# Down-projections of six first-MLP units as 2x2 block multiplications with 7 products, two units adding up in the same banks, one operand kept in DRAM

## The chip, the cores and the metric

One core of one Trainium2 chip runs the whole program. The metric is the device time of one execution in microseconds, the median of several runs. TensorE (PE) multiplies, VectorE (DVE), ScalarE (ACT) and GpSimd (POOL) work on elements, and SyncE's queue (SP) issues almost all DMAs.

## What is computed

Two layers are applied to 32 sequences of 64 tokens, 512 features each. A layer is a block and then an adapter. The block, cut to what matters here:

```python
attn_out = softmax(q k^T * scale) v @ Wp + bp
cms_out  = gelu(attn_out @ cW1 + cb1) @ cW2 + cb2          # "first MLP", 512 -> 2048 -> 512
cms_out  = cms_out + one_hot(target_codes)
modifier = gelu(concat[attn_out, cms_out] @ mW1 + mb1) @ mW2 + mb2   # "second MLP", 1024 -> 2048 -> 512
out      = clip(x + cms_out + modifier, 0, 1)
```

The adapter picks one of three small two-layer networks by sequence, adds its input and normalises. Everything is float32. The kernel reaches that accuracy by splitting each operand into a rounded high part and the rest (HI and LO, type fp32r) and by adding three products, HI*HI, HI*LO and LO*HI, in PSUM.

## The kernel before

The sequences are done in two halves of 1024 tokens, each through two layers: four **passes**, p = 0 to 3. A pass is attention, then the two MLPs, then the adapter. In the MLPs the 2048 hidden features are cut into 8 groups of 256. A group of one MLP is a **unit**: units 0 to 7 belong to the first MLP, 8 to 15 to the second.

- **The up-projection** of a unit (`term`, `terms`) multiplies a 2x2 block matrix of weights with a 2x2 block matrix of tokens. It forms 7 products, P1 to P7, of sums and differences of blocks, instead of 8; units 0 and 8 (`plain`) use 8. A product is 6 matmuls of 128x512 in the first MLP, 12 in the second. ACT copies between banks (`copy_p1`, `copy_p5`, `copy_u2`) and DVE additions (`make_z22`, `make_z12`) put the products together. Two gelu instructions on ACT (`hidden`) write the high part and the raw value of each of four 128x512 blocks H00, H11, H10, H01, and DVE subtracts to get the low part.
- **The down-projection** of units 0 to 8 and 15 (`down`) is plain: 8 products of 6 matmuls, each into its own bank of the four in `d_out`, each added to `acc` by DVE (`add`, 128x512). Units 9 to 14 (`FAST`) use 7 products of 6 matmuls into double banks `d_a` and `d_b` (`fast_down`), with six additions of 128x1024 (`fast_add`), one ACT copy of a double bank (`copy_down`), and sums of hidden blocks (`hidden_sum`, with `split_sum` on ACT and `low_sum` on DVE for their parts) and of weight blocks (`combine_down` on POOL, `split_part` on ACT, `low_part` on DVE).
- **Weights** come by DMA, one unit ahead: `w1c` and `w1m` for the up-projection, `w2` for the down-projection. POOL forms the four weight sums of each unit (`combine`). ACT writes the high part (`weight_part`, `down_part`), DVE the low part.

Each engine runs its own list in the written order. PE alternates between the products of unit u and the down-projection of unit u-1 (`mlps`), so that others prepare one while it multiplies the other:

```python
terms(p, u, P1, P5, P6); down(p, u - 1, 0); terms(p, u, P2)
terms(p, u, P7);         down(p, u - 1, 1); terms(p, u, P4, P3)
```

SP waits for the low part of the last weight operand (P3) of unit u, loads the up-projection weights of unit u+1 over them, waits for the low part of the down-projection weights and loads those of unit u+1.

## Time and profile before

| | |
|---|---|
| median of 3 runs | 2037.12 us (2036.31 to 2037.77) |
| profiled execution | 2037.42 us |
| its span (first to last instruction) | 2035.5 us |
| granted TensorE clock over the span | 0.999 |
| busy: PE, PEld, DVE, ACT, POOL | 2021.2, 1692.2, 1508.2, 1021.5, 370.0 us |
| moved by DMA | 169.78 MB, 83 GB/s over the span |

PE is the matmul row, PEld the weight loads that run beside it. A busy PE is one that has matmuls in flight. The table of the chain that ended last gives PE 95% of the span, 88% of it to line 672, the matmuls of all projections. Line 1430 is DVE's helper for every low part, so its rows are told apart by the tile names: `hs` and `t` hidden blocks, `wsc` and `wsm` up-projection weights, `wd` and `wdp` down-projection weights.

### The profile page before, as it was taken

The numbers are of one execution on the slowest core, as the hardware profiler recorded it, in microseconds if no ns is written. First come the engines' busy times: TensorE is split into PE (matmuls) and PEld (weight loads), VectorE is DVE, ScalarE is ACT, GpSimd is POOL, SyncE is SP. The second block draws the span as 40 slices with busy tenths as digits, with TensorE's granted clock in tenths as the row PEclk, the third lists the DMA queues.
The fourth block names the chain that finished last, engine by engine and source line by source line (L and its number), as shares of the span: only waits on it lengthen the run. The fifth ranks groups of instructions, "written<-read, shape, count | busy, mean of one in ns | idle before, by whom it ended". The sixth has DMA issues, their size and how long they took to land.

```text
span 2035.5 us, 27682 instructions
## 1 busy us (share of the span) xinstructions
PE 2021.2 (99%) x9500; PEld 1692.2 (83%) x9500; DVE 1508.2 (74%) x2321; ACT 1021.5 (50%) x1844; POOL 370.0 (18%) x415
## 2 busy tenths in 40 slices
PE   9999999999999999999999999999999999999998
PEld 7888888888888888888888888888888888888887
DVE  7576677888767667888867666888886766778887
ACT  5464454555356444555435444555544544445552
POOL 0011112321101102232110110223210111032321
PEclk9999999999999999999999999999999999999999
DMA  8411211213411111112460121122252021211143
GB/s 292 166 32 42 73 47 63 73 59 113 161 68 42 52 65 60 48 62 73 155 234 22 51 63 67 37 73 73 71 189 104 11 62 42 78 62 47 62 145 95
DMA packets 42377, 169.78 MB, mean 83 GB/s; under 512 B 5624, under 2 KB 9720, under 8 KB 34808
## 3 DMA queue, kind: packets, MB, share of 16 engines
q1 hardware_dynamic: 42096, 167.97, 23.8%
q8 instruction: 80, 1.31, 0.3%
q14 instruction: 57, 0.47, 0.1%
q10 hardware_dynamic: 144, 0.03, 0.0%
HBM read 146.97 MB, written 21.01 MB: 83 GB/s over the span
## 4 chain that ended last, share of the span: by engine, by line
PE 95%; DMA 2%; DVE 2%; SPq 0%; issue 0%; POOL 0%; ACT 0%; DVEq 0%; ACTq 0%
PE psum L672 88%; DMA gains<-roles_in 1%; PE psum L966 1%; PE psum L1003 1%; PE psum L747 1%; PE psum L769 1%; DVE yt L1908 0%; PE psum L770 0%; PE psum L749 0%; SPq L422 0%; DMA fraw<-fuse_in 0%; PE psum L979 0%; PE psum L991 0%; DVE stats L1889 0%; PE psum L1015 0%
## 5 line engine op out<-in xcount | busy, mean ns | idle before, releaser
L672 PE MATMUL psum<-hs,wd 128*128 128x512 f32 x1920 | 448.8, 389 | 0.5
L672 PEld LDWEIGHTS psum<-hs,wd 128*128 128x128 f32 x1920 | 360.1, 188 | 76.9 <-DVE acc L1703 2.2
L672 PE MATMUL psum<-cop,wsm 128*128 128x512 f32 x1416 | 354.7, 389 | 0.0
L672 PE MATMUL psum<-aop,wsm 128*128 128x512 f32 x1320 | 333.0, 389 | 0.0
L672 PEld LDWEIGHTS psum<-cop,wsm 128*128 128x128 f32 x1416 | 265.8, 188 | 55.2
L672 PE MATMUL psum<-aop,wsc 128*128 128x512 f32 x1320 | 311.3, 389 | 0.0
L672 PEld LDWEIGHTS psum<-aop,wsm 128*128 128x128 f32 x1320 | 247.8, 188 | 51.4
L672 PEld LDWEIGHTS psum<-aop,wsc 128*128 128x128 f32 x1320 | 247.5, 188 | 51.4
L1679 DVE TENSOR_TENSOR acc<-psum,acc 128x1024 f32<-128x1024 f32 x144 | 175.6, 1219 | 87.2 <-PE psum L672 87.1
L1703 DVE TENSOR_TENSOR acc<-psum,acc 128x512 f32<-128x512 f32 x256 | 167.9, 684 | 84.5 <-PE psum L672 84.4
L1430 DVE TENSOR_TENSOR hs<-hs_raw,hs 128x512 fp32r<-128x512 f32 x256 | 178.8, 706 | 43.5 <-ACT hs_raw L1243 43.5
L1242 ACT ACTIVATE hs<-psum,bias 128x512 fp32r<-128x512 f32 x120 | 82.1, 684 | 237.2 <-PE psum L672 237.1
L672 PE MATMUL psum<-hs,wdp 128*128 128x512 f32 x576 | 146.2, 389 | 0.0
L1242 ACT ACTIVATE hs<-zt,bias 128x512 fp32r<-128x512 f32 x112 | 81.0, 723 | 113.7 <-PE psum L672 71.7
L672 PEld LDWEIGHTS psum<-hs,wdp 128*128 128x128 f32 x576 | 108.1, 188 | 22.4
L1171 ACT ACTIVATE wsm<-w1m 128x512 fp32r<-128x512 f32 x156 | 96.1, 622 | 37.0 <-DMA w1m<-m_in 37.0
L1430 DVE TENSOR_TENSOR wsm<-w1m,wsm 128x512 fp32r<-128x512 f32 x156 | 110.3, 723 | 1.3 <-ACT wsm L1171 1.0
L672 PE MATMUL psum<-t,wdp 128*128 128x512 f32 x432 | 109.6, 389 | 0.0
L1685 DVE TENSOR_TENSOR zt<-psum,zt 128x512 f32<-128x512 f32 x56 | 38.7, 691 | 80.2 <-PE psum L672 80.2
L609 POOL TENSOR_TENSOR comb<-w1c 128x256 f32<-128x256 f32 x28 | 20.7, 738 | 416.2 <-DMA w1c<-c_in 416.2
L672 PEld LDWEIGHTS psum<-t,wdp 128*128 128x128 f32 x432 | 81.1, 188 | 16.8
L616 POOL TENSOR_TENSOR w1m<-w1m,comb 128x512 f32<-128x512 f32 x28 | 45.4, 1620 | 269.8 <-DVE wsm L1430 269.8
(193 smaller groups left out, 3072.9 us busy)
## 6 DMA issues: line engine op xcount, KB each, us to landing
w1m<-m_in SPq DMA_DIRECT2D x32, 1024.0 KB, 4.9
w1c<-c_in SPq DMA_DIRECT2D x32, 512.0 KB, 3.5
w<-c_in SPq DMA_DIRECT2D x32, 512.0 KB, 3.6
w<-m_in SPq DMA_DIRECT2D x32, 512.0 KB, 3.5
gains<-roles_in SPq DMA_DIRECT2D x30, 512.0 KB, 5.1
fw<-fused SPq DMA_DIRECT2D x6, 2048.0 KB, 10.3
fused<-fw SPq DMA_DIRECT2D x4, 2048.0 KB, 7.6
xmid<-x SPq DMA_DIRECT2D x4, 2048.0 KB, 6.8
```

The lines of the kernel that those rows point to most:

```text
L609: nc.gpsimd.tensor_tensor(st, w_block(u, 1, 0), w_block(u, 1, 1), ALU.add).then_inc(w1_sums, 1)
L616: nc.gpsimd.tensor_tensor(w_block(u, 0, 1), w_block(u, 0, 1), st, ALU.subtract).then_inc(w1_sums, 1)
L672: mm = nc.tensor.matmul(out, lhs(a), rhs(b), start=(start and n == 0), stop=(stop and n == total - 1), skip_group_check=reopened)
L747: nc.tensor.matmul(out, tq[:, j // 2, HI, j % 2, i * P:(i + 1) * P], xs[:, :, j, tile], start=(j == 0), stop=False)
L769: nc.tensor.matmul(out, val[:, HI, v_cols], val[:, :, p_cols], start=True, stop=False)
L966: nc.tensor.matmul(out, tokens, wdn_flat[:, bass.ds(role * (2 * KC * BN) + (c * KC + k) * BN, BN)], start=(b == 0 and k == 0 and a == c), ...
L1171: nc.scalar.activation(slot(u, i)[:, HI, :], w_source(u, i), ACT.Copy).then_inc(s_hi[i], 1)
L1242: nc.scalar.activation(hs[:, b, HI, m, :], h_source(h, u), ACT.Gelu, bias=b1)
L1430: return nc.vector.tensor_tensor(out, a, hi.bitcast(F32), ALU.subtract)
L1679: nc.vector.tensor_tensor(dst, bank, dst, ALU.add).then_inc(acc_done, 1)
L1685: nc.vector.tensor_tensor(zt[:, 2, :], bank_b()[:, :], zt[:, 2, :], ALU.add).then_inc(z22_done, 1)
L1703: nc.vector.tensor_tensor(dst, d_out[o][:, :], dst, ALU.add).then_inc(acc_done, 1)
```

## The change

- **Pairs.** Units 1 to 6 form three pairs (1,2), (3,4), (5,6), `PAIRED`. The down-projections of a pair are done together in the 7-product form: each of 7 products takes 12 matmuls (2 banks, 2 units, 3 parts), both units adding up in the same double bank. The six additions to `acc`, the copy and the bank turns are done once for a pair.
- **Room.** The hidden operands of two units of a pair stand in `pairs`, over the area of `cop`. One operand of that area (`x12`, attention output kept for unit 8) goes to DRAM (`kept`) in unit 0 and comes back after the last pair. The weight operands of a pair turn through 7 slots, `wdc`, in an area that unit 8's plain weights use after them. A second raw buffer `w2b` holds the odd unit's down weights; SP loads both units' raw weights together.
- **POOL** gets 4 sums per unit for the down weights, two of them formed in the slot itself (`pair_first`, `pair_last`).
- **Order.** PE's list is written anew for units 1 to 7. The lists of ACT and DVE for these units are written out one item after the other (`first_units`, 166 and 201 items); only their first lines stand here. The second MLP is as before. The softmax's five semaphores become one counter, with the same waits.
- **SP** waits for all seven low parts before it overwrites weights. Before unit 8's `w1m`, it also waits for the last pair's low parts and loads `w2` of unit 7 first.

```diff
+PAIR_DOWN = (P5, P3, P1, P6, P2, P7, P4)
+PAIRED = range(1, NG - 1)
+PAIR_SLOTS = 7
...
+        def group(u):
+            return ((u, u + 1) if u % 2 else (u - 1, u)) if paired(u) else (u,)
...
+            if paired(u):
+                return 7 * (group(u)[0] - 1) + 2 * down_turn(u, i) + (u % 2 == 0)
...
@@ SP, one_pass
                         else:
-                            sp.wait_ge(s_lo[P3], strassen(p, u) + 1)
+                            for i in range(7):
+                                sp.wait_ge(s_lo[i], units(p, u, i) + 1)
+                        if u + 1 == NG:
+                            sp.wait_ge(d_lo, d_at(p, u))
+                            load_w2(u)
                         load_w1(u + 1)
...
+                    if paired(u):
+                        if u in (4, 6):
+                            sp.wait_ge(d_lo, d_at(p, u - 1))
+                            for v in group(u):
+                                load_w2(v)
+                    elif u == 0:
+                        sp.wait_ge(d_lo, d_at(p, u + 1))
+                        load_w2(2)
+                        sp.wait_ge(x12_lo, 2 * p + 1)
+                        sp.dma_start(kept, x12_flat).then_inc(x12_stored, 16)
+                    else:
+                        sp.wait_ge(d_lo, d_at(p, u + 1))
+                        if u == NG - 1:
+                            sp.wait_ge(dn_done, dn_at(p, u))
+                            sp.wait_ge(x12_stored, 16 * (p + 1))
+                            sp.dma_start(x12_flat, kept).then_inc(x12_back, 16)
...
@@ POOL
+            def pair_first(p, u):
+                for v in group(u):
+                    pool.wait_ge(*w2_here(p, v))
+                    nc.gpsimd.tensor_tensor(w2_block(v, 2, 1), w2_block(v, 1, 1), w2_block(v, 2, 1), ALU.subtract).then_inc(w2_sums, 1)
+                    pool.wait_ge(w2_sums, w2_sum(p, v, P7))
+                    nc.gpsimd.tensor_tensor(part_source(v, P6), w2_block(v, 2, 2), w2_block(v, 2, 1), ALU.subtract).then_inc(w2_sums, 1)
+            def pair_last(p, u):
+                for i in (P5, P3):
+                    for v in group(u):
...
+                        elif u in (5, 7):
+                            combine_first(p, u)
+                            pair_first(p, u - 1)
+                            combine_last(p, u)
+                            pair_last(p, u - 1)
...
@@ PE, fast_down
+                        pe.wait_ge(acc_done, {P5: a0 - (2 if behind(u) is None else 1), P3: a0 + 1, P1: a0 + 2, P7: a0 + 3, P4: a0 + down_turn(u, P7)}[i])
...
+                        mm = product(out[:, o, :], [(lambda a, v=v: part(v, i)[:, a, o * P:(o + 1) * P],
+                                                     lambda c, v=v: h_operand(v, i, c), None) for v in us], first, True, not first)
...
@@ PE, mlps
-                    if fast(u - 1):
+                    if u in (1, 2):
+                        terms(p, u, P1, P5, P6)
+                        down(p, 0, u - 1, 0, 1)
+                        terms(p, u, P2, P7)
+                        down(p, 0, u - 1, 2, 3)
+                        terms(p, u, P4, P3)
+                    elif u in (3, 5):
+                        terms(p, u, P1, P5, P6)
+                        fast_down(p, u - 1, P5)
+                        terms(p, u, P2, P7)
+                        fast_down(p, u - 1, P3)
+                        terms(p, u, P4, P3)
+                    elif u in (4, 6):
+                        terms(p, u, P1)
+                        fast_down(p, u - 2, P1)
+                        terms(p, u, P5, P6)
+                        fast_down(p, u - 2, P6)
+                        terms(p, u, P2)
+                        fast_down(p, u - 2, P2)
+                        terms(p, u, P7)
+                        fast_down(p, u - 2, P7)
+                        terms(p, u, P4, P3)
+                        fast_down(p, u - 2, P4)
+                    elif u == NG - 1:
+                        terms(p, u, P1, P5, P6)
+                        fast_down(p, u - 1, P5)
+                        terms(p, u, P2)
+                        fast_down(p, u - 1, P3)
+                        terms(p, u, P7)
+                        fast_down(p, u - 1, P1)
+                        terms(p, u, P4)
+                        fast_down(p, u - 1, P6, P2, P7)
+                        terms(p, u, P3)
+                        fast_down(p, u - 1, P4)
...
@@ ACT, weight_part
                 if u == NG:
+                    act.wait_ge(dn_done, dn_at(p, NG - 2) + down_turn(NG - 2, {P6: P2, P7: P7, P2: P4, P4: P4}[i]) + 1)
...
@@ DVE
+            def first_units(p, layer):
+                weight_part(p, 1, P4)
+                weight_part(p, 1, P3)
+                add(p, layer, 0, 0, 0)
+                make_z22(p, 1)
...
```

How PE's list stands in unit 7 of pass 0, before. The `aop,wsc` rows are up-projection products (6 matmuls: a first one with its waits, then 5), the `hs,wd` rows the plain down-projection of unit 6.

```order
L672 MATMUL psum<-aop,wsc 128x512 [waits p1_copied,s_lo1]
L672 MATMUL psum<-aop,wsc 128x512 x5
L672 MATMUL psum<-aop,wsc 128x512 [waits u2_copied,s_lo6]
L672 MATMUL psum<-aop,wsc 128x512 x5
L672 MATMUL psum<-hs,wd 128x512 [waits h_lo3,acc_done]
L672 MATMUL psum<-hs,wd 128x512 x2
L672 MATMUL psum<-hs,wd 128x512 [waits h_lo1]
L672 MATMUL psum<-hs,wd 128x512 x2
L672 MATMUL psum<-hs,wd 128x512 [waits acc_done]
L672 MATMUL psum<-hs,wd 128x512 x5
```

The same place after the change: the pair product P5 of units 5 and 6 (12 matmuls), then P2 of unit 7, then the pair product P3.

```order
L831 MATMUL psum<-pairs,wdc 128x512 [waits ht_lo,d_lo,acc_done]
L831 MATMUL psum<-pairs,wdc 128x512 x2
L831 MATMUL psum<-hs,wdc 128x512 x3
L831 MATMUL psum<-pairs,wdc 128x512 x3
L831 MATMUL psum<-hs,wdc 128x512 x3
L831 MATMUL psum<-aop,wsc 128x512 [waits p1_copied,s_lo1]
L831 MATMUL psum<-aop,wsc 128x512 x5
L831 MATMUL psum<-pairs,wdc 128x512 [waits h_lo0,d_lo,acc_done]
```

Six matmuls now stand between a pair product and the next one that waits for `acc_done`, DVE's addition of it; before, several products of other banks lay between such a wait and what it waits for.

SP's list from the load of unit 7's up-projection weights on, before:

```order
L483 DMA w1c<-c_in 128x1024 [waits s_lo2]
L487 DMA w_52<-c_in 128x1024 [waits d_lo]
L481 DMA w1m<-m_in 128x2048 [waits s_lo2]
L487 DMA w_52<-m_in 128x1024 [waits d_lo]
L481 DMA w1m<-m_in 128x2048 [waits s_lo3]
```

And after the change (`w_52` is `w2`; the first row stands for the loads of units 6 and 7):

```order
L583 DMA w1c<-c_in 128x1024 [waits s_lo4,s_lo3,s_lo5,s_lo2,s_lo6,s_lo1,s_lo0] x2
L587 DMA w2b<-c_in 128x1024 [waits d_lo]
L587 DMA w_52<-c_in 128x1024
L587 DMA w_52<-c_in 128x1024 [waits s_lo4,s_lo5,s_lo3,s_lo6,s_lo2,d_lo,s_lo1,s_lo0]
L581 DMA w1m<-m_in 128x2048
L660 DMA cop<-kept 128x2048 [waits x12_stored,dn_done,d_lo]
L587 DMA w_52<-m_in 128x1024
L581 DMA w1m<-m_in 128x2048 [waits s_lo3]
```

The load of unit 8's `w1m` moved behind `d_lo`, the low part of the last weight operand of pair (5,6), and behind a load of `w2`; the return of `kept` is new, ahead of unit 8's `w2`.

## Rows read from the trace of the kernel before

**Rows 1.** The page: busy time of the engines, and the granted clock in 40 slices.

```profile
PE 2021.2 (99%) x9500; PEld 1692.2 (83%) x9500; DVE 1508.2 (74%) x2321; ACT 1021.5 (50%) x1844; POOL 370.0 (18%) x415
...
PEclk9999999999999999999999999999999999999999
```

**Rows 2.** The chain that ended last, pass 0: start us, us, what.

```profile
121.92 380.81 PE psum L672 x1680
```

**Rows 3.** Who PE waited for, whole span: us in total, times, longest us.

```profile
PE psum L991 <- DVE hz L1430: 3.6, 4, 1.6
PE psum L679 <- POOL ident L581: 1.5, 1, 1.5
```

**Rows 4.** Stretches of pass 0: units 1 to 7, then units 8 to 15.

```profile
core 0: us, PE busy (x) PEld busy (x) DVE busy (x) ACT busy (x) POOL busy (x), PEclk, DMA share, GB/s
121.92:264.55 142.63, 142.63 (x630) 118.12 (x630) 95.98 (x159) 70.96 (x136) 19.47 (x25) 1.00 0.17 52
264.55:502.70 238.15, 238.15 (x1052) 197.28 (x1051) 191.28 (x260) 125.50 (x219) 60.92 (x53) 1.00 0.22 76
```

**Rows 5.** DVE in order of time, unit 11: start us, us, what [idle before].

```profile
378.08 0.42 DVE L1430 TENSOR_TENSOR wdp<-comb,wdp 128x256 fp32r<-128x256 f32 x1
378.42 0.68 DVE L1430 TENSOR_TENSOR wsm<-comb,wsm 128x512 fp32r<-128x512 f32 x1
379.02 1.22 DVE L1679 TENSOR_TENSOR acc<-psum,acc 128x1024 f32<-128x1024 f32 x1
380.15 0.60 DVE L1430 TENSOR_TENSOR wdp<-w,wdp 128x256 fp32r<-128x256 f32 x1
```

**Rows 6.** PE in order of time, unit 10 and the end of unit 15.

```profile
342.07 1.52 PE L672 MATMUL psum<-t,wdp 128*128 128x512 f32 x6
343.43 1.52 PE L672 MATMUL psum<-aop,wsm 128*128 128x512 f32 x6
...
498.47 11.50 PE L672 MATMUL psum<-hs,wd 128*128 128x512 f32 x48
```

**Rows 7.** PEld in order of time, the same two places.

```profile
343.21 1.32 PEld L672 LDWEIGHTS psum<-aop,wsm 128*128 128x128 f32 x6
...
504.20 1.93 PEld L672 LDWEIGHTS psum<-hs,wd 128*128 128x128 f32 x9 [0.55 <-DVE acc L1703]
```

**Rows 8.** DVE in order of time, the same two places.

```profile
343.70 1.22 DVE L1679 TENSOR_TENSOR acc<-psum,acc 128x1024 f32<-128x1024 f32 x1 [2.11 <-PE psum L672]
...
503.45 2.49 DVE L1703 TENSOR_TENSOR acc<-psum,acc 128x512 f32<-128x512 f32 x4
```

**Rows 9.** ACT in order of time, units 11 and 12.

```profile
377.71 0.40 ACT L1194 ACTIVATE wdp<-w 128x256 fp32r<-128x256 f32 x1
...
383.20 0.63 ACT L1199 ACTIVATE t<-t_raw 128x512 fp32r<-128x512 f32 x1 [0.24 <-DVE t_raw L1665]
...
396.67 1.01 ACT L1205 ACTIVATE psum<-psum 128x1024 f32<-128x1024 f32 x1 [0.24 <-PE psum L672]
```

**Rows 10.** POOL in order of time, first and second MLP.

```profile
171.12 0.74 POOL L609 TENSOR_TENSOR comb<-w1c 128x256 f32<-128x256 f32 x1 [12.75 <-DMA w1c<-c_in]
...
290.06 2.21 POOL L613 TENSOR_TENSOR comb<-comb,w1m 128x512 f32<-128x512 f32 x1 [15.56 <-DVE wsm L1430]
```

**Rows 11.** DVE in order of time, at the second POOL row.

```profile
289.90 1.22 DVE L1430 TENSOR_TENSOR cop<-cop_raw,cop 128x1024 fp32r<-128x1024 f32 x1
291.04 1.78 DVE L1430 TENSOR_TENSOR hs<-hs_raw,hs 128x512 fp32r<-128x512 f32 x1
```

**Rows 12.** The page, DMA issues: KB each, median us to landing.

```profile
w1m<-m_in SPq DMA_DIRECT2D x32, 1024.0 KB, 4.9
...
w<-c_in SPq DMA_DIRECT2D x32, 512.0 KB, 3.6
...
xmid<-x SPq DMA_DIRECT2D x4, 2048.0 KB, 6.8
```

**Rows 13.** SP's queue in order of time, the load for unit 8.

```profile
249.24 0.33 SPq L481 DMA_DIRECT2D w1m<-m_in  x1
```

More of the change, by code:

```diff
@@ new lines, in part_at, with w2_block, w2_odd, w2_here @@
+        def part_at(p, u, i):
+            if paired(u):
+                return d_at(p, group(u)[1]) + 2 * down_turn(u, i) + (u % 2 == 0) + 1
+            return d_at(p, u) + down_turn(u, i) + 1
+        def w2_block(u, half, chunk):
+            return (w2b if w2_odd(u) else w2)[:, (2 - chunk) * V + (half - 1) * 2 * P:(2 - chunk) * V + half * 2 * P]
+        def w2_odd(u):
+            return paired(u) and u % 2 == 1
+        def w2_here(p, u):
+            loads = [v for v in range(u + 1) if w2_odd(v) == w2_odd(u)]
+            per_pass = sum(w2_odd(v) == w2_odd(u) for v in range(UNITS))
+            return w2b_loaded if w2_odd(u) else w2_loaded, 16 * (per_pass * p + len(loads))
@@ L790, in block_products @@
                     pe.wait_ge(s_lo[PLAIN[m, k]], n + 1)
-                    if b == 0:
+                    if kind and which == 0 and b and k == 0:
+                        pe.wait_ge(x12_back, 16 * (p + 1))
+                    elif b == 0:
                         pe.wait_ge(op_lo[(P1, P2)[k]], 2 * p + which + 1)
@@ L866, in down @@
                         pe.wait_ge(acc_done, acc_at(p, u) + o + 1)
-                    elif fast(u - 1):
+                    elif behind(u) is not None:
                         pe.wait_ge(acc_done, acc_at(p, u) - (o < 2))
@@ L1308, in second_unit @@
+            def mlps(p, layer):
+                first_unit(p, layer, 0)
+                first_units(p, layer)
+                first_unit(p, layer, 1)
+                for u in range(NG + 1, UNITS):
+                    second_unit(p, layer, u)
             def second_unit(p, layer, u):
@@ L1783, in second_unit @@
+            def mlps(p, layer):
+                first_unit(p, layer, 0)
+                first_units(p, layer)
+                first_unit(p, layer, 1)
+                for u in range(NG + 1, UNITS):
+                    second_unit(p, layer, u)
             def second_unit(p, layer, u):
```

687 lines of the change are left out of this document (542 added, 145 removed).

## Prediction

> **What bounds the kernel now.** I read the page first: PE is busy for 99% of the span at the full granted clock [rows 1]. A busy PE need not be a bound one, so I next read the chain in order of time. The reader should see one unbroken piece of PE in pass 0, from 121.92 us, 380.81 us long, of 1680 matmuls; the other three passes show a piece of the same length and count [rows 2]. That is units 1 to 15 but for the last two thirds of unit 15's down-projection. It gives 380.81/1680 = 0.2267 us for each matmul, with nothing else in it. The waits say the same: the largest of PE's is 3.6 us in the whole run, in the adapter [rows 3]. So in the MLPs a matmul saved is 0.2267 us saved, as long as the others still deliver in time. The stretches show what room they have: in units 1 to 7 PE runs 630 matmuls in 142.63 us, beside 95.98 us of DVE, 70.96 of ACT and 19.47 of POOL [rows 4].
>
> **What is removed.** A plain down-projection is 48 matmuls, a share in a pair is 42. Six units in four passes: 6 x 6 x 4 = 144 matmuls, 144 x 0.2267 = **32.6 us**, all on the path. Units 1 to 7 become 594 matmuls, 134.7 us a pass.
>
> **What DVE gets.** Starts that follow each other directly show what an instruction occupies: 0.34 us for 256 columns, 0.60 for 512, 1.13 for 1024 [rows 5]. By the new list, units 1 to 7 hold 86 of 256 columns (44 parts of up weights, 42 of down weights), 96 of 512 (8 additions, 14 z blocks, 24 sums of hidden blocks, 24 and 22 low parts, 4 parts for unit 8) and 19 of 1024 (18 additions, one weight block). That is 29.2 + 57.6 + 21.5 = 108.3 us in 134.7, 80%. It fits, and from each item that waits for a PE product to the next one that PE needs, the sum of the items between stays under PE's time between, except at the places priced below. Cost nothing, cover 26 us a pass; if that is gone, DVE becomes the bound (rival 3).
>
> **What ACT gets.** Add 42 casts of 256 columns at 0.40, 24 of 512 at 0.63 and 3 copies at 1.01 [rows 9] to the 70.96 us: 106 us at most (the six weight casts and six gelus it loses are left in), 79% of 134.7. Hidden. POOL: 28 sums as before and 24 new, 52 x 0.74 = 38.5 us [rows 10]. Hidden as work; what it does to DVE is rival 3.
>
> **What is added on the path: four short turns in unit 7.** The last pair has only unit 7 to hide in. There the pair products P5, P3 and P1 are 6 matmuls apart, and so are P7 and P4. Each of these waits for DVE's addition of the product before it in the same double bank (P6 waits for ACT's copy of P1). Unit 10 shows how long such a turn takes. A 6-matmul product starts at 342.07 and the next one at 343.43 [rows 6]; its addition starts at 343.70, 0.27 later, and lasts 1.22 [rows 8]. At the end of unit 15 a weight load starts 0.06 us after an addition ends (503.45 plus 0.69 for the first of four, then 504.20) [rows 7, 8]. A weight load runs 0.22 us ahead of its matmul (343.21 against 343.43) [rows 6, 7]. Together 0.27 + 1.22 + 0.06 + 0.22 = 1.77 us, and 6 matmuls cover 1.36: 0.41 us late, three times. With the copy (0.24 after its product, 1.01 long [rows 9]) it is 1.53 against 1.36: 0.17. Sum 1.4 us a pass, **5.6 us**. The bounds: nothing, if the modelled ends are late by that much, and 0.55 a turn, the idle time of the one real stall of this kind [rows 7], 8.8 us. I take 5.6, since that stall costs its row of 48 matmuls 11.50 - 11.04 = 0.46 us [rows 6] and the same sum of steps explains it. Elsewhere pair products have 12 or more matmuls, or other banks, in between: nothing.
>
> **The gate of unit 8.** SP now loads `w1m` of unit 8 behind the low part of the last pair operand, whose slot comes free only when pair product P6 ends. From there: 0.27 to ACT, 0.40 and 0.42 for the two parts [rows 5, 9], some 0.4 to issue two loads, then 1.5 MB. The 1 MB load alone takes 4.9 us, 2 MB take 6.8 [rows 12]; I take 6.5. Then two casts and two low parts of 512, some 2.0. That is 10.0 us. PE reaches unit 8 after P2, P7, P3 of unit 7 and P4: 42 matmuls, 9.5 us, plus 0.4 for P4's turn. Before, the load was issued at 249.24 [rows 13], 15 us ahead. Nearly even: late by 0 to 2 us a pass; I take 0.3, **1.2 us**. The next items (unit 8's other two parts, unit 7's last hidden blocks and its weight block) follow within 0.5 us of their time each, no more.
>
> **The operand in DRAM.** 1 MB out in unit 0, waited for by the gelu of H10 in unit 1, some 20 us later; 1 MB back, issued once unit 7's weight block is split, some 5 us after the last pair product, and needed 72 matmuls (16.3 us) after it. The nearest loads take 4.9 and 6.8 us [rows 12]: hidden with 4 us to spare. If it came late, unit 8 would wait for the excess, 0 to 2 us a pass. Moved loads of `w2` arrive 5 us before POOL needs them for pairs (3,4) and (5,6); the load of unit 8's `w2` is 5 us later than before and 15 us early. The softmax's one counter for five changes no wait: nothing.
>
> **Small lateness.** Lists this full, in fixed order, will now and then hold an item that PE waits for behind one that is waiting itself (the copy of P1 in unit 5 behind a weight part that hangs on POOL, for one). Nothing in the trace of before prices it: from below nothing, from above the 26 us that DVE has free being used up, which is rival 3. I take 0.5 us a pass, **2.0 us**, near the lower end, since before DVE is 80% busy in units 8 to 15 (191.28 of 238.15 [rows 4]) and PE loses nothing there.
>
> **Sum.** 32.6 - 5.6 - 1.2 - 2.0 = 23.8. The profiled execution took 2037.4 us (its span is 2035.5; it stands 0.3 above the median of the runs): **2013.5 us**.
>
> **Rival 1: all of it is hidden.** The turns cost nothing because a matmul's end is modelled, and the load arrives. For it: 1680 matmuls without a gap under the same kinds of waits [rows 2]. Against it: the stall at 504.20 [rows 7]. 2037.4 - 32.6 = 2004.8 us.
>
> **Rival 2: full lists, more waiting.** The cross waits of ACT, DVE and POOL cost 3 us a pass instead of 0.5, and the load for unit 8 is 1.5 us late. 2004.8 + 5.6 + 12 + 6 = 2028 us.
>
> **Rival 3: DVE becomes the bound, by POOL's reads.** At 290.06 a POOL addition starts inside DVE's 1.22 us low part at 289.90, which runs its normal time; the POOL one takes 2.21 us, and DVE's next low part, from 291.04, takes 1.78 instead of 0.68 [rows 5, 10, 11]. So one waits for the other, and DVE loses 1.1 us to an instruction of 1.3. If each of the 52 POOL sums of units 1 to 7 cost DVE its full 0.74 us, DVE would need 108.3 + 38.5 = 146.8 us where PE took 142.63 before: 4.2 us a pass longer, 17 us in all, **2054 us, slower**. The point from which it decides is 69% of POOL's time lost by DVE (26.4 of 38.5 us), and slower than before from 89%. Against it: an addition that reads PSUM beside POOL keeps its time, nearly a third of DVE's new time is of that kind (8 + 14 instructions of 512 and 18 of 1024), and before, DVE kept 80% busy without PE losing any. The Trainium skill, page "SBUF — State Buffer", section on who interferes with whom, says that the shared ports are an exclusive lock: a DVE instruction with both inputs in SBUF and a GpSimd one that reads SBUF block each other fully, whoever came first. By that rule, and the trace agrees (2.21 and 1.78 us), each such meeting costs what rival 3 takes; the rule alone says nothing of how often they meet.
>
> **Rival 4: a load in the new SP order is far too late.** SP is one queue, and it now waits for down weights before up weights. If the return of `kept` or unit 8's weights came 6 to 8 us late in each pass, the gain would be gone: 2035 to 2041 us. Against it, the sums above leave it 0 to 2.
>
> **How the numbers follow.** The forecast with its own range of 2008 to 2020 has 0.47, rival 1 (2003 to 2008) 0.24, rival 2 (2020 to 2033) 0.18, rival 4 0.04, rival 3 0.07. The predicted time is the likeliest case, 2013.5. With 2 in 10 left out, the range runs from 2004, rival 1 with its full saving, to 2027, most of rival 2. 0.2% is 4 us, about what a measurement of this kernel can tell from no change. Faster by more: 0.89, which is the forecast with rivals 1 and 2; within it: 0.03, most of rival 4; slower: 0.08, rival 3 and the end of rival 4.
>
> **What the profile of the changed kernel would show.** PE has 144 matmuls fewer, 9356. The long piece of each pass falls from 380.81 us to some 375, broken in unit 7. Weight loads before pair products P3, P1 and P4 of unit 7 are idle by 0.3 to 0.6 us, released by DVE's 1024 additions, and P6's by ACT's copy. DVE is 80 to 90% busy in units 1 to 7. If PE shows no idle time there, rival 1 holds. If its idle time is released by DVE low parts all over units 3 to 7, and these last longer than 0.42 and 0.68 us beside POOL, it is rival 3. If it is released by the DMA of `w1m` or of `cop`, it is the gate or rival 4. A time above 2027 or below 2004 makes the prediction wrong.

## The result, and the profile after

| | before | after |
|---|---|---|
| median of the runs, us | 2036.8 (2036.31 to 2037.77, 4 runs) | 2024.47 (2023.48 to 2025.08, 4 runs) |
| profiled execution: time, span, us | 2037.4, 2035.5 | 2024.03, 2022.3 |
| PE's matmuls | 9500 | 9356 |
| DVE busy, us | 1508.2 (74%) | 1631.7 (81%) |

The ratio is 0.9937, 95% interval 0.9923 to 0.995: faster by 12 us, where 32.6 us of matmuls went. 2013.5 was forecast and the stated range, 2004 to 2027, held; of the 23.8 us of gain that I had taken as likeliest, about half came. One of the four runs of version e10 further down took 3774.6 us at a granted clock of 0.831, where all others had 0.998 or more; e10's ratio leaves it out (the other three: 2011.34 to 2012.03, median 2011.44), its median of 2011.74 does not. The page after, beside [rows 1]:

```profile
PE 1998.4 (99%) x9356; PEld 1662.8 (82%) x9356; DVE 1631.7 (81%) x2513; ACT 1104.6 (55%) x2072; POOL 472.6 (23%) x511
...
PEclk9999999999999999999999999999999999999999
```

The clock is as before. The chain that ended last (start us, us, what) was one piece of 380.81 us [rows 2]. Now, in pass 0 and at the start of pass 1's second MLP:

```profile
130.92 5.77 PE psum L831 x24
141.32 42.48 PE psum L831 x186
197.42 42.49 PE psum L831 x186
239.96 4.34 PE psum L831 x18
244.35 13.94 PE psum L831 x60
258.35 241.00 PE psum L831 x1062
...
743.51 7.03 DMA w1m<-m_in
```

From 258.35, where the last pair product P4 starts, PE runs on unbroken; all that is lost in pass 0 is lost in units 1 to 7. From the start of unit 1 to PE's restart at the end of unit 15, the passes took 382.28 us each before (121.92 to 504.20 in the first), and take 378.67, 379.84, 378.62 and 378.45 now. That is 3.61, 2.44, 3.66 and 3.83 us less, 13.5 in all, where 36 matmuls less should give 8.16 each.

PE's weight loads show where (pass 0; start us, us, what [idle ahead of it <- what ended it]):

```profile
130.92 1.23 PEld L831 LDWEIGHTS psum<-aop,wsc 128*128 128x128 f32 x6 [1.04 <-DVE wsc L1786]
...
141.32 1.22 PEld L831 LDWEIGHTS psum<-aop,wsc 128*128 128x128 f32 x6 [0.99 <-DVE wsc L1786]
...
189.55 2.61 PEld L831 LDWEIGHTS psum<-pairs,wdc 128*128 128x128 f32 x12 [0.74 <-issue]
...
195.27 1.23 PEld L831 LDWEIGHTS psum<-aop,wsc 128*128 128x128 f32 x6 [0.39 <-issue]
197.39 0.53 PEld L831 LDWEIGHTS psum<-hs,wdc 128*128 128x128 f32 x3 [0.90 <-DVE wdc L1786]
...
239.93 0.53 PEld L831 LDWEIGHTS psum<-pairs,wdc 128*128 128x128 f32 x3 [0.44 <-issue]
...
258.31 0.53 PEld L831 LDWEIGHTS psum<-pairs,wdc 128*128 128x128 f32 x3 [0.44 <-issue]
```

0.04 us of each idle time is the usual step from load to load. These are, in order: unit 1 before P7; unit 2 before P6; the pair product P4 of (1,2), which waits for DVE's addition of the pair product P7; unit 5's P6; the pair product P5 of (3,4); and two of unit 7's turns (a turn is the change of a double bank from one product to the next). A load can run ahead of its matmul, so PE itself loses a little less. By the starts of its matmuls against 0.2267 us each, pass 0 loses 1.77 us in units 1 and 2, 1.67 in units 4 and 5, 1.07 in unit 7: 4.51 us, and 8.16 - 4.51 = 3.65 is the gain of pass 0. The first five places are in all four passes. Unit 8's load costs 1.24 us in pass 1 (the DMA piece in the chain above) and nothing in the others.

At the same place before, DVE's three low parts of unit 1 stood like this (start us, us, what):

```profile
129.68 1.08 DVE L1430 TENSOR_TENSOR wsc<-w1c,wsc 128x256 fp32r<-128x256 f32 x3
```

And now, with POOL beside them:

```profile
128.28 1.71 DVE L1786 TENSOR_TENSOR aop<-aop_raw,aop 128x1024 fp32r<-128x1024 f32 x1 [0.19 <-ACT aop L1331]
129.92 2.71 DVE L1786 TENSOR_TENSOR wsc<-w1c,wsc 128x256 fp32r<-128x256 f32 x3
```

```profile
128.87 1.71 POOL L765 TENSOR_TENSOR w2b<-w2b 128x256 f32<-128x256 f32 x1
130.66 0.80 POOL L767 TENSOR_TENSOR comb2p<-w2b 128x256 f32<-128x256 f32 x1
...
135.29 0.75 POOL L779 TENSOR_TENSOR wdc_raw<-w,comb2p 128x256 f32<-128x256 f32 x1
```

Three low parts of 256 columns took 1.08 us before; they take 2.71 beside the pair sums, which POOL forms in one burst of eight. The third of them is the weight operand of P7, and all seven must be done before SP loads unit 2's weights. In units 4 and 5 the burst runs from 184.75 to 195.3, and there DVE is busy 31.13 of 32.00 us (stretch, us, then PE, PEld, DVE, ACT, POOL with counts, clock, DMA):

```profile
183.00:215.00 32.00, 31.16 (x136) 24.88 (x135) 31.13 (x49) 23.01 (x49) 13.30 (x13) 1.00 0.14 48
```

The two theories to part. T1: POOL's sums, which read SBUF, stretch DVE's instructions with two SBUF inputs, and that makes the stalls of units 1, 2, 4 and 5. T2: no collision is needed; PE's new order and fuller lists are enough.

### The profile page after: what moved, and what is told of

The parts are those of the page before. It is cut to its first block, busy times and chain, and to the rows that moved or that the text cites. A ratio compares the mean times of both kernels' runs of the same rounds, so it can differ in the third digit from the quotient of the medians.

```text
span 2022.3 us, 28718 instructions
## 1 busy us (share of the span) xinstructions
PE 1998.4 (99%) x9356; PEld 1662.8 (82%) x9356; DVE 1631.7 (81%) x2513; ACT 1104.6 (55%) x2072; POOL 472.6 (23%) x511
## 4 chain that ended last, share of the span: by engine, by line
PE 90%; DVE 4%; DMA 2%; issue 1%; ACT 1%; SPq 1%; POOL 1%; DVEq 0%; ACTq 0%
PE psum L831 83%; PE psum L1160 1%; DMA gains<-roles_in 1%; PE psum L1197 1%; PE psum L906 1%; PE psum L928 1%; DVE wsc L1786 1%; DVE pairs_raw L2022 0%; DVE yt L2454 0%; PE psum L1173 0%; DMA fraw<-fuse_in 0%; PE psum L929 0%; PE psum L908 0%; SPq L522 0%; DVE pairs L1786 0%
## 5 line engine op out<-in xcount | busy, mean ns | idle before, releaser
L2038 DVE TENSOR_TENSOR acc<-psum,acc 128x1024 f32<-128x1024 f32 x216 | 263.4, 1220 | 103.2 <-PE psum L831 102.7
L831 PE MATMUL psum<-aop,wsc 128*128 128x512 f32 x1320 | 319.9, 390 | 5.0 <-DVE wsc L1786 4.8
L831 PE MATMUL psum<-hs,wd 128*128 128x512 f32 x768 | 181.3, 390 | 0.5
L831 PE MATMUL psum<-pairs,wdc 128*128 128x512 f32 x672 | 177.0, 392 | 1.7 <-DVE acc L2038 1.1
L831 PEld LDWEIGHTS psum<-hs,wd 128*128 128x128 f32 x768 | 143.9, 188 | 32.2 <-DVE acc L2062 2.2
L831 PEld LDWEIGHTS psum<-pairs,wdc 128*128 128x128 f32 x672 | 124.5, 188 | 34.0 <-issue 8.2
L1786 DVE TENSOR_TENSOR hs<-hs_raw,hs 128x512 fp32r<-128x512 f32 x192 | 133.4, 707 | 11.4 <-ACT hs_raw L1446 11.4
L1445 ACT ACTIVATE hs<-psum,bias 128x512 fp32r<-128x512 f32 x80 | 54.9, 687 | 88.0 <-PE psum L831 87.8
L734 POOL TENSOR_TENSOR comb<-w1c 128x256 f32<-128x256 f32 x28 | 26.1, 932 | 300.8 <-DMA w1c<-c_in 300.7
L831 PE MATMUL psum<-fw,xs 128*128 128x512 f32 x384 | 93.1, 395 | 0.0
```

Of the source, the lines that this page charges most:

```text
L734: nc.gpsimd.tensor_tensor(st, w_block(u, 1, 0), w_block(u, 1, 1), ALU.add).then_inc(w1_sums, 1)
L831: mm = nc.tensor.matmul(out, lhs(a), rhs(b), start=(start and n == 0), stop=(stop and n == total - 1), skip_group_check=reopened)
L1445: nc.scalar.activation(h_high(u, h), h_source(h, u), ACT.Gelu, bias=b1)
L1786: return nc.vector.tensor_tensor(out, a, hi.bitcast(F32), ALU.subtract)
L2038: nc.vector.tensor_tensor(dst, bank, dst, ALU.add).then_inc(acc_done, 1)
```

## The experiments

In the expectations, P1 to P7 are called parts. The last column sums all idle time ahead of PE's weight loads in the four MLP stretches, beyond 0.04 us each: 22.5 us for the change, of which PE itself loses 19.1.

| run | median (range), us | ratio to before, 95% | idle, us |
|---|---|---|---|
| the change | 2024.47 (2023.48 to 2025.08) | 0.9937, 0.9923 to 0.995 | 22.5 |
| e1_write_only | 2014.68 (2012.6 to 2017.12) | 0.9894, 0.9879 to 0.991 | 10.3 |
| e2_pool_later | 2031.49 (2029.41 to 2032.93) | 0.9969, 0.9957 to 0.9981 | 32.4 |
| e3_unit1_order | 2027.92 (2025.86 to 2030.3) | 0.9958, 0.9944 to 0.9971 | 24.5 |
| e4_halves | 2022.85 (2022.7 to 2024.7) | 0.9933, 0.9919 to 0.9946 | 19.6 |
| e5_early_sums | 2023.25 (2020.05 to 2023.56) | 0.9926, 0.9913 to 0.994 | 18.5 |
| e6_vector_sums | 2025.61 (2024.26 to 2028.11) | 0.9945, 0.9931 to 0.9958 | 22.5 |
| e7_cover | 2025.94 (2024.08 to 2027.81) | 0.9944, 0.9931 to 0.9958 | 24.4 |
| e8_together | 2017.42 (2016.66 to 2017.75) | 0.9901, 0.9886 to 0.9916 | 14.7 |
| e9_lists | 2012.71 (2011.9 to 2013.82) | 0.9881, 0.9866 to 0.9896 | 8.1 |
| e10_pool_sums | 2011.74 (from 2011.34) | 0.9875, 0.9857 to 0.9894 | 8.3 |
| e11_lists45 | 2023.11 (2022.12 to 2025.55) | 0.9934, 0.992 to 0.9947 | 21.1 |
| e12_last_wait | 2012.16 (2009.75 to 2013.86) | 0.9878, 0.9861 to 0.9894 | 8.0 |

Intervals are some 3 us to each side, so differences of 2 us between neighbours rest on the trace and not on the time.

**Sums that read nothing.** In `pair_first` and `pair_last`:

```diff
-nc.gpsimd.tensor_tensor(part_source(v, P6), w2_block(v, 2, 2), w2_block(v, 2, 1), ALU.subtract).then_inc(w2_sums, 1)
+nc.gpsimd.memset(part_source(v, P6), 0.0).then_inc(w2_sums, 1)
...
```

> POOL's eight pair sums of each pair of units are written as constants (memsets), so they read nothing from SBUF; the sums of the down-projection's weights are left out of what is computed. Waits, order and counts of instructions stay. In the profile of the changed kernel TensorE loses 4.5 us in a pass: 1.77 in units 1 and 2, 1.67 in units 4 and 5, 1.07 at the turns of unit 7. Theory T1, the stalls of units 1, 2, 4 and 5 come from POOL's pair sums that read SBUF beside VectorE's low parts and stretch them (0.42 us to 0.9): with nothing read they go but for about 0.45 a pass that is due to the order of unit 1 alone, so 3.0 a pass and 12 us less, about 2012.5 us, with the turns of unit 7 unchanged at 1.07. Rival T2, the order of TensorE's products and the fuller lists alone make VectorE late: the stalls stay within 1 us a pass of what they are and the time is 2021 to 2025 us.

2014.68 us, 9.8 less; the idle time falls by 12.2 us. POOL's memsets and DVE's three low parts beside them:

```profile
130.13 0.57 POOL L777 MEMSET wdc_raw<- 128x256 f32 x2
130.63 0.57 POOL L779 MEMSET wdc_raw<- 128x256 f32 x2
```

```profile
129.94 1.08 DVE L1786 TENSOR_TENSOR wsc<-w1c,wsc 128x256 fp32r<-128x256 f32 x3
```

1.08 us again, with POOL writing all the while. SP issues unit 2's load at 131.16 instead of 132.76. The waits of units 4 and 5 are gone altogether; of 1.00 and 0.95 in units 1 and 2, 0.47 and 0.72 stay; the turns are unchanged. T1 holds, and T2 keeps a share of 1.2 us a pass. A memset is also shorter than a sum (0.3 against 0.74 us), so the time alone can't tell reading from length; the unstretched low parts beside running memsets can. The Trainium skill, page "SBUF — State Buffer", section "Who interferes with whom", says just this: a DVE instruction with two SBUF inputs meets a GpSimd instruction that reads SBUF, not one that only writes it. The trace agrees, 1.08 against 2.71 us.

In units 4 and 5 the same 22 instructions of DVE, from the z block at 183.83 in the change up to the addition at 199.03, can be laid side by side. First the change, then e1:

```profile
183.83 0.69 DVE L2044 TENSOR_TENSOR zt<-psum,zt 128x512 f32<-128x512 f32 x1
...
185.23 1.04 DVE L1786 TENSOR_TENSOR t<-zt,t 128x512 fp32r<-128x512 f32 x1
...
187.34 0.96 DVE L1786 TENSOR_TENSOR wsc<-w1c,wsc 128x256 fp32r<-128x256 f32 x1
```

```profile
183.07 0.69 DVE L2044 TENSOR_TENSOR zt<-psum,zt 128x512 f32<-128x512 f32 x1
...
184.47 0.69 DVE L1786 TENSOR_TENSOR t<-zt,t 128x512 fp32r<-128x512 f32 x1
...
186.18 0.42 DVE L1786 TENSOR_TENSOR wsc<-w1c,wsc 128x256 fp32r<-128x256 f32 x1
...
195.69 1.21 DVE L2038 TENSOR_TENSOR acc<-psum,acc 128x1024 f32<-128x1024 f32 x1
```

From the z block's start to the start of that addition (199.03 and 195.69) it is 15.20 us in the change and 12.62 in e1, though e1 has 0.41 us of idle time in it and the change none above 0.15. So DVE did not wait for POOL's results there: its own instructions were longer beside the sums, by more than the 1.90 us that PE waited.

**The burst later.** POOL's sums of pair (1,2) go behind unit 2's combinations, the splits of its part 5 with them:

```diff
                         if u == 1:
                             combine(p, u)
-                            pair_first(p, u)
-                            pair_last(p, u)
+                        elif u == 2:
+                            combine(p, u)
+                            pair_first(p, u)
+                            pair_last(p, u)
```

> Everything is computed. POOL forms the sums of pair (1, 2) behind unit 2's combinations of weights instead of ahead of them, and the split of that pair's part 5 on ACT and VectorE moves behind those of unit 1, directly ahead of unit 2's own. T1 (collision in the burst beside unit 1): the burst at 128 to 136 us no longer meets unit 1's low parts, the combinations of unit 2 and ACT's copies come earlier, and of the 1.77 a pass in units 1 and 2 some 1.3 go, 5 us in all, about 2019.5 us; units 4 and 5 keep their 1.67. T2 (order alone): 0 to 1 us less. A third outcome: the burst meets the low parts of unit 2 or 3 instead and the stalls only move, 2022 to 2026 us.

2031.49 us, 7 more: the third outcome, and worse than its bound. Units 1 and 2 keep 0.46 and 0.72 as in e1, but the burst (139.68 to 147.9) now meets the low parts that unit 3 and the first pair need:

```profile
143.76 1.22 DVE L1788 TENSOR_TENSOR pairs<-pairs_raw,pairs 128x512 fp32r<-128x512 f32 x1
```

```profile
150.99 5.29 PEld L833 LDWEIGHTS psum<-aop,wsc 128*128 128x128 f32 x24 [1.55 <-issue]
157.01 1.22 PEld L833 LDWEIGHTS psum<-aop,wsc 128*128 128x128 f32 x6 [0.72 <-issue]
```

1.22 us where 0.68 is normal. From 139.3 to 150 us DVE has no idle time above 0.15 us in which it could make this up; in unit 1 of the change it had some (0.33 us before 135.35 and 0.56 before 136.60).

**Unit 1 in the old order.**

```diff
-                        down(p, 0, u - 1, 0, 1)
-                        terms(p, u, P2, P7)
-                        down(p, 0, u - 1, 2, 3)
+                        down(p, 0, 0)
+                        terms(p, u, P2, P7)
```

> Everything is computed. In unit 1 alone TensorE's order is the one of before: all four outputs of unit 0's last down product between parts 6 and 2, where the change has two there and two later, which brings part 7 forward by 12 matmuls or 2.7 us. T1: VectorE's third low part is in time again in spite of its 2.71 us beside POOL (it was 0.91 late with 2.7 to gain), so the 0.91 goes, and with it the load that waits for it comes up to 0.9 earlier and unit 2's 0.86 goes for the most part: 5 to 7 us less in all, 2017.5 to 2019.5 us. T2 gives the same here; if neither order nor collision is the cause, nothing changes (2023 to 2025 us). The stretch of VectorE's low part beside POOL (2.71 us) stays, which tells cause from cover.

2027.92 us, 3.5 more: a miss for all I expected. P7's wait is gone, but another stands in its place, before P4 (PE's load, then DVE's addition that it waits for):

```profile
136.53 5.29 PEld L831 LDWEIGHTS psum<-aop,wsc 128*128 128x128 f32 x24 [1.72 <-issue]
```

```profile
135.77 0.69 DVE L2048 TENSOR_TENSOR zt<-psum,zt 128x512 f32<-128x512 f32 x1 [1.68 <-ACT zt L1416]
```

P7 goes through ACT's copy and DVE's z22 before its bank is free for P4: 1.7 us, ending at 136.46. Before, this stood behind 24 down matmuls of unit 0; in the change units 1 and 2 have 24 each instead of 48, since their pair's down work comes later. So the edit was no undoing of the order: half of what covered the two gaps is no longer there, and it can cover one or the other.

**The turns in halves.** For the last pair, DVE's additions of P5, P3 and P7 and ACT's copy are made in two halves of 512, and PE waits for each half:

```diff
+nc.vector.tensor_tensor(dst[:, 0, :], bank[:, 0, :], dst[:, 0, :], ALU.add).then_inc(acc_first, 1)
+nc.vector.tensor_tensor(dst[:, 1, :], bank[:, 1, :], dst[:, 1, :], ALU.add).then_inc(acc_done, 1)
```

> Everything is computed. In the last joint pair alone, VectorE's three additions of parts 5, 3 and 7 into the partial results and ACT's copy of the banks are made in two halves of 512 columns, each with its own signal, and TensorE waits for each half before it writes that half. If the turns of unit 7 cost what the changed kernel's profile shows (1.07 us a pass: 0.30 or so at each of three waits for VectorE and 0.05 at ACT's copy), the waits for the first half end about 0.6 us earlier and all of it goes: 4.3 us less, about 2020.2 us. If TensorE's idle time there is only a wait that would be paid again behind it, at the next turn, the time stays at 2023 to 2025 us. The stalls of units 1, 2, 4 and 5 stay.

2022.85 us, 1.6 less, not 4.3. The idle time at the turns is gone in all passes, but PE is then earlier at unit 8, and in three of four passes it waits for the weights there, by 0.26, 1.90 and 1.39 us where it was 0, 1.24 and 0 (the second of them):

```profile
751.59 2.38 PEld L832 LDWEIGHTS psum<-aop,wsm 128*128 128x128 f32 x11 [1.94 <-issue]
```

The idle time falls by 2.9 us in all. So the turns do cost what PE's starts say, and half of it is paid again at the gate, the load for unit 8.

**The burst earlier.** In unit 0 POOL waits 26 us and DVE's list is thin:

```diff
-                            combine(p, u)
+                            combine_two(p, u)
                             pair_first(p, u)
                             pair_last(p, u)
+                            combine_third(p, u)
+                            combine_last(p, u)
```

> Everything is computed. POOL forms the eight sums of pair (1, 2) in unit 0, between its second and third combination for unit 1 (after 91 us, where it waits 26 us in the changed kernel and VectorE's list is thin), instead of at 128 us beside unit 1's low parts. T1 (collision): unit 1's third low part takes 1.1 us again instead of 2.7, the load behind it is issued at 131.2 us as with sums that read nothing, and the stalls of units 1 and 2 go from 0.91 and 0.86 to what that run kept, 0.47 and 0.72: 0.6 to 0.8 a pass, 2.4 to 3.2 us in all, about 2021.5 us. T2 (order and full lists, no collision): no change, 2023 to 2025 us. The 0.47 and 0.72 that stay are the share of the order in both.

```profile
130.28 1.24 PEld L841 LDWEIGHTS psum<-aop,wsc 128*128 128x128 f32 x6 [0.50 <-DVE wsc L1796]
```

The low parts take 1.08 us again, SP issues at 131.04, and units 1 and 2 lose 0.46 and 0.72, within 0.01 us what e1 kept. The idle time falls by 4.0 us, 3.1 of them in units 1 and 2. The median says 1.2 less, which by its number is T2's case; the span of the profiled execution says 3.1 (2019.2). That is too little to show in the time, and the trace decides. It is the same collision taken away with everything computed. As the whole burst is gone from unit 1, this run by itself does not part POOL's reads from its length; e1's low parts beside memsets do.

**Four sums of pair (3,4) on DVE.**

```diff
@@ POOL
-                            pair_last(p, u - 1)
+                            if u == 7:
+                                pair_last(p, u - 1)
...
@@ DVE
                 weight_part(p, 5, P2)
+                pair_sums(p, 4)
                 hidden_sum(p, 4, P5)
```

> Everything is computed. The last four of the eight sums of pair (3, 4), parts 5 and 3, are made by VectorE (0.42 us each, 1.7 in all) behind its low part of unit 5's part 2, instead of by POOL at 191 to 195 us. T1: VectorE pays 1.7 us of its own but its neighbours keep their nominal times (0.95 back to 0.42 twice, 1.23 to 0.68, 1.83 to 1.2 for a pair), so units 4 and 5 lose about 0.6 to 0.8 a pass instead of 1.67, since the first four sums on POOL still meet VectorE ahead of them: 3.5 to 4 us less, about 2020.5 us. T2 (VectorE's list is simply too full there): 1.7 us more on it make the stalls of units 4 and 5 longer by up to 1.7 a pass, 2025 to 2031 us.

2025.61 us: no gain, T2's case by its number. The pair product's wait is gone (0.85), but unit 5's P6 waits 1.35 instead of 0.35, since ACT's queue stands behind a hidden sum that DVE reaches later:

```profile
192.50 0.63 ACT L1394 ACTIVATE pairs<-pairs_raw 128x512 fp32r<-128x512 f32 x1 [3.69 <-DVE pairs_raw L2023]
```

DVE's own four sums, 1.7 us by their nominal times and 2.2 here, cost as much as the collision that they replace.

**One output on each side of P7**, in units 1 and 2:

```diff
-                        terms(p, u, P2, P7)
-                        down(p, 0, u - 1, 2, 3)
+                        terms(p, u, P2)
+                        down(p, 0, u - 1, 2)
+                        terms(p, u, P7)
+                        down(p, 0, u - 1, 3)
```

> Everything is computed. In units 1 and 2 the last two outputs of unit 0's down-projection are no longer both between parts 7 and 4: one stands ahead of part 7 (6 matmuls, 1.36 us), one stays behind it. The run with four outputs ahead of part 2 and none behind part 7 showed a wait of 1.68 us ahead of part 4, with nothing to cover it. If each gap is a matter of how many matmuls of the down-projection stand ahead of it, part 7 is no longer late (0.91 and 0.86 gone) and part 4 waits 1.68 less 1.36, 0.3 each: 1.2 less a pass, 4.7 us in all, about 2019.8 us. If the delay is only handed on (VectorE is late through the unit, whatever PE does), the time stays at 2023 to 2027 us.

2025.94 us. P7 and P4 of unit 1 wait no more, but unit 2 waits three times instead of once, 2.06 us in place of 0.95, and unit 3 once, 0.35:

```profile
136.45 1.23 PEld L831 LDWEIGHTS psum<-aop,wsc 128*128 128x128 f32 x6 [0.57 <-DVE wsc L1788]
137.93 1.22 PEld L831 LDWEIGHTS psum<-aop,wsc 128*128 128x128 f32 x6 [0.26 <-DVE wsc L1788]
140.50 1.22 PEld L831 LDWEIGHTS psum<-aop,wsc 128*128 128x128 f32 x6 [1.35 <-DVE wsc L1788]
```

DVE's three low parts still take 2.72 us here, so unit 2's weights come late, and PE only meets them sooner. The delay is handed on, as long as the collision stands.

**Together.** e5, e6, e7 and e4, and at SP:

```diff
                         if u + 1 == NG:
-                            sp.wait_ge(d_lo, d_at(p, u))
-                            load_w2(u)
+                            sp.wait_ge(d_lo, part_at(p, 5, P4))
                         load_w1(u + 1)
+                        if u + 1 == NG:
+                            sp.wait_ge(d_lo, d_at(p, u))
+                            load_w2(u)
```

> Everything is computed. The last three edits and the halves of the turns together, and the load of unit 8's weights of part 1 ahead of that of unit 7's down weights, so that it is issued 1 us earlier. If the causes add up, a pass loses 0.6 in units 1 and 2, 0.6 in units 4 and 5, nothing at the turns and under 0.5 at the load of unit 8, in place of 4.5: about 2010 to 2012 us, which would beat the changed kernel by 0.6 to 0.7%. If the edits get in each other's way (VectorE's list holds more instructions in unit 7 and 4), 2016 to 2022 us.

2017.42 us, the second case: 7 us less, and 7.8 us less of idle time. The places say which edits gave it. The turns' idle time is gone, 5.7 us, and with the load issued earlier unit 8 takes only 0.3 more; so e4's gain now stays. Units 1 to 3 have 3.6 us less, of which e5 alone gave 3.1. Units 4 to 6 have 1.2 more. So e6 and e7, which gave nothing alone, give little or nothing here too: with the burst gone, the split cover takes away unit 1's last wait, 0.46 us a pass, but 0.35 appears in unit 3, and in units 4 and 5 a pass loses 2.06 us where the change loses 1.90.

**With the lists mended.** On top of that four list entries moved, DVE's four sums parted two and two, and the outputs parted in unit 1 alone. Three of the moves:

```diff
+                weight_part(p, 2, P5)
                 hidden_sum(p, 1, P5)
-                weight_part(p, 2, P5)
...
-                weight_part(p, 5, P1)
                 fast_add(p, 2, P7)
+                weight_part(p, 5, P1)
...
+                copy_p1(p, 5)
                 split_part(p, 3, P5)
...
-                copy_p1(p, 5)
                 split_part(p, 3, P3)
```

> Everything is computed. As the version of all edits together (2017.4 us, still 3.6 us lost a pass: 0.73 ahead of unit 2's part 6, 0.36 in unit 3, 0.71 behind unit 4's part 7, 1.36 ahead of unit 5's part 6, 0.42 at unit 8), with the moves that its profile asks for. VectorE's low part of unit 2's part 5, on which POOL's third combination and so part 6 waits, goes ahead of a sum of hidden units; its low part of unit 5's part 1 goes behind the addition of part 7; its own four sums of pair (3, 4) are parted two and two; ACT's copy of part 1's bank in unit 5 goes ahead of two copies that wait for those sums; ACT's copy of unit 7's down weights goes behind two of unit 8's; the two outputs are parted in unit 1 alone. If each wait is made by the list entry ahead of it, all five go: 2 to 3.5 us a pass, 2004 to 2009 us. If they are only handed to the next wait (VectorE as the bound of these units), 2012 to 2018 us.

> Everything is computed. As the kernel before it in this call, but the sums of pair (3, 4) are all POOL's again, as in the change. If the collision of POOL's sums with VectorE is what makes part 5 of that pair late, 0.85 a pass comes back there (3.4 us more than the run with VectorE's sums). If only the order of the lists mattered, the two are within 1 us of each other, or this one is faster by VectorE's 1.7 us a pass where that list is full.

2012.71 and 2011.74 us, the second case of e9's expectation: the waits of units 2, 3, 5 and 8 fall from 0.73, 0.36, 1.36 and 0.42 to 0.26 and nothing in pass 0, that of 0.70 before the pair product P4 of (1,2) goes too, and one of 1.42 is left, before the pair product P5 of (3,4). It is 1.42 with DVE's sums and with POOL's. So e10's second case holds: who forms those four sums makes no difference here. Either way DVE is as full: it is busy for 31.20 of the 32 us from 183 to 215 in e9, and 31.39 in e10. e10 is the fastest in this study with e12, 0.9875 against the change's 0.9937, 0.6% below it.

**Two list entries alone**, on the change as it was (the last two moves above):

> Everything is computed. The changed kernel with two moves alone, both at units 4 and 5, and POOL's sums where they are: VectorE's low part of unit 5's part 1 behind its addition of part 7, and ACT's copy of part 1's bank in unit 5 ahead of the copies that wait for POOL's sums. If the 0.70 and 0.35 a pass there are made by the entries ahead of them, which the collision stretched, they go and the 0.85 ahead of the pair's part 5 stays or grows by some of it: 0.5 to 1.05 a pass, 2 to 4 us less, 2020.5 to 2022.5 us. If VectorE is simply too full there, nothing changes (2023 to 2026 us).

2023.11 us. The 0.70 and 0.35 go and 0.85 becomes 1.44: of 1.90 us of idle time in units 4 and 5 of pass 0, 0.46 is won and the rest is handed to the next product. The time is that of the second outcome, the trace shows the first.

**The last wait.** On top of e10, for pair (3,4):

```diff
+                low_sum(p, 4, P5)
                 low_part(p, 3, P5)
-                hidden(p, 3, H00)
                 low_part(p, 4, P5)
-                low_sum(p, 4, P5)
+                hidden(p, 4, H11)
+                hidden(p, 3, H00)
```

> Everything is computed. As the fastest version so far (2011.7 us, POOL's sums of pair (3, 4) where the change has them, 1.68 us lost in pass 0), with moves at its largest wait, 1.42 us a pass ahead of pair (3, 4)'s part 5: VectorE's low half of the summed hidden units for part 5 and its two low parts of that part's weights go ahead of the low halves of two other blocks of hidden units (1.22 us and 0.68 us), and ACT copies the second unit's part 5 ahead of two activations. POOL's collision stays as it is. If a late list entry only has to be moved out of the wait, the 1.42 goes: 5.7 us less, about 2006 us, within 2 us of the 2004.2 us that 144 matmuls less give. If VectorE is the bound there, beside POOL, the wait goes to the next product or to the sum's other parts, and the time stays within 1.5 us of 2011.7 us.

2012.16 us: no gain. The 1.42 becomes 0.17, and 1.28 us stand behind it:

```profile
193.54 0.53 PEld L844 LDWEIGHTS psum<-hs,wdc 128*128 128x128 f32 x3 [0.21 <-DVE wdc L1818]
...
199.29 0.53 PEld L844 LDWEIGHTS psum<-hs,wdc 128*128 128x128 f32 x3 [0.41 <-DVE wdc L1818]
...
210.52 1.24 PEld L844 LDWEIGHTS psum<-aop,wsc 128*128 128x128 f32 x6 [0.47 <-DVE wsc L1818]
212.29 0.53 PEld L844 LDWEIGHTS psum<-t,wdc 128*128 128x128 f32 x3 [0.52 <-issue]
```

In this stretch DVE is busy for 31.34 of 32 us:

```profile
183.00:215.00 32.00, 31.81 (x138) 25.21 (x137) 31.34 (x52) 23.75 (x51) 12.67 (x13) 1.00 0.08 22
```

With DVE this full, the lists of e9 to e12 all leave 1.4 to 2.2 us of idle time a pass in units 3 to 6. That no other order does better was not shown.

## Why the prediction was right, and where it was not

- **The saving.** 144 matmuls less at 0.2267 us: 9356 in the trace, and the stretches of four passes that add up to 32.6 less the idle time. Right.
- **Four short turns, 5.6 us.** Too dear. Measured 1.07 us of PE's time a pass, 4.3 in all. The three turns at DVE's additions behind P5, P3 and P7 cost 0.30 to 0.32, where 0.41 was worked out; the one at ACT's copy 0.09, where it was 0.17; 0.05 stand before the first. The mechanism stands, 0.1 us too dear each. e4 takes the turns away, though half of it comes back at unit 8.
- **The gate of unit 8, 1.2 us.** 1.24 in all, but as one wait in pass 1 and none in the others. The sum was right by luck of the mean; "nearly even" is what the trace shows, and e4 shows how steep it is: PE 1 us earlier there, 2.3 us more of waiting in all.
- **ACT, the operand in DRAM, the moved loads, at nothing.** ACT copied P1 late in unit 5, but behind entries that wait for POOL. No wait of PE ends with the return of `kept`. It was not tried without it.
- **DVE's list "fits", at nothing, and small lateness, 2.0 us.** This is the step that failed. The prediction said that "the sum of the items between stays under PE's time between" and showed no row for it. What this step should hold is 32.6 - 13.5 - 4.3 - 1.2 = 13.6 us, 3.4 a pass, at five places that are the same in every pass. Two things were missed. First, I priced DVE at 108.3 us in 134.7. In the trace it is busy 123.63 of 136.21 us:

```profile
122.14:258.35 136.21, 134.03 (x584) 108.25 (x582) 123.63 (x202) 89.74 (x189) 44.22 (x49) 1.00 0.15 51
```

  91%, not 80. Not all of that is stretch. My prices, put on the 159 instructions of units 1 to 7 before (47 of 256 columns, 101 of 512, 11 of 1024), give 89.0 us, where the trace has 95.98 [rows 4], so they come out 7 us low even there. In e1, with no new reads, the same 202 instructions are busy for 116.9 us; the new reads add the other 6.7. What decided was a stretch that the mean of units 1 to 7 hid. From 183 to 215 us DVE was busy for 19.79 of 32 us before, is busy for 31.13 in the change, and for 29.92 in e1, where PE does not wait once:

```profile
183.00:215.00 32.00, 32.00 (x143) 26.50 (x142) 29.92 (x54) 24.95 (x54) 7.39 (x13) 1.00 0.13 43
```

  Second, POOL's new sums come in bursts of eight, just where DVE's low parts are due. e1 takes the reads away and with them 12.2 of 22.5 us of idle time; of the 15.4 us at the five places, 10.7 go. e5 takes the first burst alone and with it 4.0 us. What was left in units 1 and 2 is order and lost cover (e3, e7), and list entries that wait ahead of due ones (e9).
- **The rivals.** The time fell into rival 2's band, its lower part, and its cause is rival 3's mechanism at a fraction of its strength: the 24 new sums of a pass, 17.8 us at 0.74, cost DVE 6.7 us by the comparison with e1, 38%, where rival 3 took all of it and 69% was the point from which it decides. I had given the collision only its extreme, where DVE becomes the bound of the whole of units 1 to 7. In truth it nearly fills one stretch, and makes due entries late elsewhere. Rival 2 had 3 us a pass of cross waits, and 3.4 were measured, but it named no cause for them, and its 6 us at unit 8 were 1.2. So the range held by the width that an unpriced lateness had given it, not by the working of the likeliest case. What I held against rival 3 stands: DVE's additions of 1024 that read PSUM took 1.22 us in the mean, the 72 beside POOL like the 144 others. Rival 1, all hidden, is off: 2004.8 us was reached by no version, 2011.74 was the nearest median. Rival 4 did not occur.
- **What I said the profile would show.** The long piece broken in unit 7: yes, but also before. DVE 80 to 90% busy: 91%. Weight loads before P3, P1 and P4 of unit 7 idle by 0.3 to 0.6 us: 0.44 each. The lines named for rival 3, idle time released by DVE's low parts that last longer beside POOL, were there, though in units 1, 2, 4 and 5 and not all over units 3 to 7: 4.8 us released by `wsc`, 2.0 by `pairs` in the waits of the whole run:

```profile
PE psum L831 <- DVE wsc L1786: 4.8, 8, 0.6
...
PE psum L831 <- DVE pairs L1786: 2.0, 4, 0.5
PE psum L831 <- DVE acc L2038: 1.1, 3, 0.4
```

What stays open: e8 joined five edits and e9 more, and only the places, not separate runs, part their shares; medians and idle times differ by 1 to 3 us in several runs (e5: 1.2 less in the one, 4.0 in the other), and no row explains it.

## What to carry to other kernels

When work moves onto an engine that was 70% busy, count its load stretch by stretch, a few products long, and not over the whole stage; and price instructions with two SBUF inputs at what they take beside POOL's sums, not alone. Place POOL's reads where DVE's list is thin, even 30 us early. When a change takes matmuls out, ask which waits those matmuls covered: taking a wait away moved all or part of it to a later product in six of these runs (e3, e4, e6, e7, e11, e12). What gave time back was a burst or its reads taken from where the list was full (e1, e5), a load issued early enough for the gain to stay (e8), and several late list entries mended at once (e9).

## What the runs showed that I had not expected

- A single edit at one of several late places can be judged by the trace, but hardly by the time: e5 took 4.0 us of idle time away and 1.2 from the median. And a sum of edits has to be read place by place: the 7 us of e8 are the gains of e4 and e5, and next to nothing of e6 and e7.
- A collision is not a sum of lengths. In unit 1 the burst's first three sums, 1.71, 0.80 and 0.92 us long, and the start of the fourth cost three low parts 1.63 us together. In e2 the same burst, 11 us later, stretched some eight instructions of DVE by about half a microsecond each and gave PE's loads 2.5 us of idle time a pass more.
- POOL's memset of 256 columns takes 0.3 us beside DVE and leaves it alone; its sum takes 0.74 to 1.7 and does not.
